# Windowed attention and two convolutions on one core: the maxima's transfer issued by ScalarE, and three engines' orders changed within a strip

## What is computed

```python
# first layer
x = layernorm2d(x0)                       # over the 96 channels of each pixel
q, k = conv1x1(x, qk_w)                   # 48 channels each
vs = conv1x1(x, vs_w)                     # 96 channels; v1 = first 48, v2 = last 48
local = depthwise_conv3x3(vs, depth_w)
q, k, v1 = roll(q, k, v1, by=-4 in both directions)
# windows of 8 x 8 pixels, 4 heads of 12 channels
y = softmax(q_window @ k_window.T * 12**-0.5) @ v_window
y = concat([roll_back(y), v2])
s = (y + local).mean(over the image)
ca = sigmoid(fu2 @ leaky_relu(fu1 @ s))
out0 = proj(y * ca + local * (1 - ca)) + x0
# second layer: pooled = out0.mean(); four taps per channel and image from pooled
out = depthwise_conv3x3(out0, taps(pooled), masked to the 4 taps above and left) + bias
```

## Time and profile before

| | before |
|---|---|
| runs | 1500.32 us median of 3 (1500.12 to 1502.79) |
| profiled execution | 1503.79 us, its span 1502.2 us |
| mean granted TensorE clock | 0.984 |
| PE / DVE / ACT / POOL busy, share of the span | 88% / 84% / 58% / 15% |
| DMA queue of SP | 202.60 MB, 53.9% of 16 engines' span |
| chain that ended last, largest parts | PE 36%, ACT 20%, DVE 16%, issue 13%, DMA 13% |

### The profile page before, as it was taken

How to read it: one execution, slowest core, us unless ns; L and a number is a source line. 1 busy time by engine, 2 the same in 40 slices (tenths; PEclk the granted TensorE clock), 3 DMA queues, 4 the chain that set the end, 5 groups by cost and what they waited for, 6 DMA issues and landing times.

```text
span 1502.2 us, 38208 instructions
## 1 busy us (share of the span) xinstructions
PE 1323.6 (88%) x12403; PEld 782.0 (52%) x12403; DVE 1263.8 (84%) x2222; ACT 875.8 (58%) x2279; POOL 230.8 (15%) x741
## 2 busy tenths in 40 slices
PE   5989898889899999989899999988989998888986
PEld 3666666555555555555555555555555555433332
DVE  3565656479999999999999999999989998999998
ACT  2566666666666666776566666765666666622221
POOL 2111111111122211221111211220112011000000
PEclk9999999999999999999999999999999999999999
DMA  2121212345665566645655566646655664678884
GB/s 62 51 82 55 81 55 81 99 98 148 167 148 144 138 152 165 156 114 154 166 147 139 138 159 156 156 114 159 155 125 141 161 155 112 164 181 195 211 199 126
DMA packets 81357, 203.07 MB, mean 135 GB/s; under 512 B 15248, under 2 KB 19112, under 8 KB 81320
## 3 DMA queue, kind: packets, MB, share of 16 engines
q1 hardware_dynamic: 81320, 202.60, 53.9%
HBM read 136.57 MB, written 64.91 MB: 134 GB/s over the span
## 4 chain that ended last, share of the span: by engine, by line
PE 36%; ACT 20%; DVE 16%; issue 13%; DMA 13%; ACTq 1%; DVEq 0%; SPq 0%; POOL 0%; POOLq 0%
DMA qd<-nmx 12%; PE banks_s L521 9%; ACT pt L811 5%; PE banks_t L529 5%; PE banks_t L483 5%; ACT km L767 4%; DVE mx L1009 4%; ACT ybuf L799 4%; PE banks_g L612 4%; PE banks_g L496 4%; DVE mixed L1181 3%; PE banks_g L614 3%; DVE oo L1192 3%; ACT vw L780 2%; DVE zs L1204 2%
## 5 line engine op out<-in xcount | busy, mean ns | idle before, releaser
L1181 DVE SCALAR_TENSOR_TENSOR mixed<-vin,c_pack,mixed 96x1024 f32<-96x1024 f32 x352 | 450.0, 1278 | 6.6
L1192 DVE SCALAR_TENSOR_TENSOR oo<-zs,l_w,oo 96x1024 f32<-96x1024 f32 x192 | 245.1, 1276 | 8.3 <-ACT oo L847 4.1
L811 ACT ACTIVATE pt<-banks_t 128x512 f32<-128x512 f32 x256 | 138.6, 593 | 129.0 <-PE banks_t L529 127.5
L1009 DVE TENSOR_REDUCE mx<-banks_s 128x8 f32<-128x512 f32 x260 | 167.6, 687 | 48.1 <-PE banks_s L521 47.3
L529 PE MATMUL banks_t<-qd,km 64*128 64x128 f32 x2048 | 152.8, 290 | 30.1 <-DMA qd<-nmx 30.0
L521 PE MATMUL banks_s<-km,qd 64*128 64x128 f32 x2080 | 152.9, 286 | 18.9 <-issue 15.2
L980 DVE BATCH_NORM_STATS2 bn<-banks_a 128x6 f32<-128x96 f32 x528 | 99.0, 249 | 80.5 <-PE banks_a L471 80.1
L521 PEld LDWEIGHTS banks_s<-km,qd 64*128 64x128 f32 x2080 | 129.7, 189 | 70.7 <-DVE mx L1009 40.4
L612 PE MATMUL banks_g<-vin,proj_t 128*96 128x512 f32 (+1 forms) x288 | 150.2, 622 | 11.4 <-DMA ycat<-y_img 5.7
L529 PEld LDWEIGHTS banks_t<-qd,km 64*128 64x128 f32 x2048 | 127.9, 192 | 49.9 <-issue 26.1
L434 POOL COPY vrow<-vw 96x16 f32<-96x16 f32 (+2 forms) x520 | 153.4, 349 | 0.0
(11 more groups left out here) (148 smaller groups left out, 1842.5 us busy)
## 6 DMA issues: line engine op xcount, KB each, us to landing
vin<-v_img SPq DMA_DIRECT2D x64, 495.0 KB, 5.9
v_img<-vrow SPq DMA_DIRECT2D x130, 198.0 KB, 2.8
xc<-in_x SPq DMA_DIRECT2D x134, 192.0 KB, 2.6
x<-in_x SPq DMA_DIRECT2D x64, 384.0 KB, 7.2
out<-oo SPq DMA_DIRECT2D x64, 384.0 KB, 3.0
y_img<-ybuf SPq DMA_DIRECT2D x128, 99.0 KB, 2.0
ycat<-v_img SPq DMA_DIRECT2D x64, 198.0 KB, 4.9
ycat<-y_img SPq DMA_DIRECT2D x64, 198.0 KB, 7.0
```

The lines of the kernel that those rows point to most:

```text
L811: fn(pt[:, 2 * r + n, :], banks_t[:, n, :], ACT.Exp).then_inc(pt_done, 1)
L1009: v.tensor_reduce(mx[:, n, :, 4 * r:4 * r + 4].rearrange("q h e -> q e h"), banks_s[:, n, :].rearrange("q (e h k) -> q e h k", h=2, k=K), ...
L1181: v.scalar_tensor_tensor(out=mb[:C, par, :, 0:W], in0=vin[:C, par, 1 + dh:1 + dh + WS, 1 + dw:1 + dw + W], scalar=depth_w[:, DVE_TAPS[m]:D ...
L1192: v.scalar_tensor_tensor(out=oo[:, par, :, :], in0=zs[:, at:at + WS, 1 + dw:1 + dw + W], scalar=l1_w[:, n:n + 1], in1=oo[:, par, :, :], op ...
```

## The change

In `strip`, the DMA of the maxima is issued by ScalarE right behind the instruction that writes them, and no more by SP behind the loads; `alone` keeps SP for it. On PE, x_transposed 1 moves up behind vs_of, project 0 goes ahead of scores 0, values 1 ahead of scores 1, and max_transposed behind project 1 (in a `gated` strip it stays ahead of it). On ACT, rsqrt goes ahead of keys. On DVE, statistics 1 and variance go ahead of mix 2, maxima 0 behind l1 (1), maxima 1 behind mix 5, and each `maxima` is one instruction over both banks; the counts on `mx_done` are halved.

```diff
@@ -343,7 +343,7 @@
 
-            def strip(h, k, attend=True, y=True, ahead=False, prev=False, older=False, gate=None):
+            def strip(h, k, attend=True, y=True, ahead=False, prev=False, older=False, gate=None, alone=False):
 
@@ -367,14 +367,14 @@
                     load_strip(t - LAG + 1, k, prev, gate)
-                if attend:
+                if attend and alone:
                     move_max(t + 1, 1 - k)
 
-            strip(0, 0, y=False)
-            strip(0, 1)
+            strip(0, 0, y=False, alone=True)
+            strip(0, 1, alone=True)
             with sp.Fori(1, NS // 2) as h:
-                strip(h, 0)
-                strip(h, 1)
+                strip(h, 0, alone=True)
+                strip(h, 1, alone=True)
             sp.wait_ge(rim_stored, 16 * 2 * B)
@@ -531,7 +531,7 @@
             def max_transposed(s):
-                pe.wait_ge(mx_done, 4 * (s + 1))
+                pe.wait_ge(mx_done, 2 * (s + 1))
                 nc.tensor.transpose(ps_mx, mx[:].rearrange("q t h p -> q (t h p)"), ident[:]).then_inc(mt_done, 1)
@@ -589,7 +589,7 @@
             scores(0, 0)
-            pe.wait_ge(mx_done, 2)
+            pe.wait_ge(mx_done, 1)
             scores(0, 1)
@@ -640,7 +640,7 @@
                 values(t, k, 0, not y)
-                pe.wait_ge(mx_done, 4 * (t + 1) + 2)
+                pe.wait_ge(mx_done, 2 * (t + 1) + 1)
                 scores(1 - k, 1)
@@ -659,6 +659,7 @@
                     vs_of(t + 1)
+                    x_transposed(t + 2, k, h + 1, 1)
                 elif prev:
@@ -672,35 +673,36 @@
                 if attend:
-                    x_transposed(t + 2, k, h + 1, 1)
                     keys_queries(t + 1)
...
                     pe.wait_ge(km_done, 2 * (t + 2))
-                    pe.wait_ge(qd_done, 2 * (t + 2))
-                    pe.wait_ge(nmx_done, t + 1)
                 if gated is not None:
                     pe.wait_ge(mid_act, gated + 1)
-                if attend:
-                    scores(1 - k, 0)
-                if gated is not None:
                     pe.wait_ge(proj_done, N_PROJ * (gated + 1) - 2)
...
                     project(u, um, par, 0, tail)
+                if attend:
+                    pe.wait_ge(qd_done, 2 * (t + 2))
+                    pe.wait_ge(nmx_done, t + 1)
+                    scores(1 - k, 0)
                 if gate is not None and not attend:
...
                 if attend:
-                    pe.wait_ge(mx_done, 4 * (t + 1) + 2)
+                    values(t, k, 1, not y)
+                    pe.wait_ge(mx_done, 2 * (t + 1) + 1)
                     scores(1 - k, 1)
-                    values(t, k, 1, not y)
                     pe.wait_ge(yq_done, FREE + 2 * t + 1)
-                    max_transposed(t + 1)
                 if gated is not None:
+                    if attend:
+                        max_transposed(t + 1)
                     one_column(gated, projT[:], st[:, 12:13], 3, C, 3)
...
                     project(u, um, par, 1, tail)
+                if attend and gated is None:
+                    max_transposed(t + 1)
                 if gate is not None and not attend:
@@ -800,10 +802,12 @@
 
-            def maxima_out(s):
+            def maxima_out(s, k):
                 act.wait_ge(mt_done, s + 1)
...
                 fn(nmx[:], ps_mx, ACT.Copy, scale=-1.0).then_inc(nmx_done, 1)
+                act.wait_ge(nmx_done, s + 1)
+                act.dma_start(qd[62:66, k, :, :, :].rearrange("j p w q -> j (p w q)"), nmx[:]).then_inc(mx_moved, 16)
 
@@ -916,8 +920,8 @@
                         sigmoid_exp(gated)
+                    rsqrt(t + 2)
                     keys(t + 1, 1 - k)
-                    rsqrt(t + 2)
                     queries(t + 1, 1 - k)
@@ -931,7 +935,7 @@
                 if attend:
-                    maxima_out(t + 1)
+                    maxima_out(t + 1, 1 - k)
                 if ahead:
@@ -1005,10 +1009,9 @@
                     dve.wait_ge(mt_done, s)
-                for n in range(2):
-                    v.tensor_reduce(mx[:, n, :, 4 * r:4 * r + 4].rearrange("q h e -> q e h"),
-                                    banks_s[:, n, :].rearrange("q (e h k) -> q e h k", h=2, k=K),
-                                    AX.X, ALU.max).then_inc(mx_done, 1)
+                v.tensor_reduce(mx[:, :, :, 4 * r:4 * r + 4].rearrange("q n h e -> q n e h"),
+                                banks_s[:, :, :].rearrange("q n (e h k) -> q n e h k", h=2, k=K),
+                                AX.X, ALU.max).then_inc(mx_done, 1)
 
@@ -1243,13 +1246,13 @@
                     mix(u, par, 1, tail)
+                if attend:
+                    statistics(t + 2, 1)
+                    variance(t + 2)
                 if gated is not None and attend:
...
                     mix(u, par, 2, tail)
-                if attend:
-                    statistics(t + 2, 1)
-                    variance(t + 2)
                 if gated is not None and attend:
@@ -1261,16 +1264,17 @@
                     normalise(t + 2, k, 1)
-                    maxima(t + 1, 0)
                 if gate is not None and not attend:
...
                 if attend:
-                    maxima(t + 1, 1)
+                    maxima(t + 1, 0)
                 if cur and not tail:
                     mix(u, par, 5, tail)
+                if attend:
+                    maxima(t + 1, 1)
                 if gate is not None and not attend:
```

## The result

The changed kernel takes **1555.43 us** (median of 4, 1547.86 to 1556.14) against 1500.32: ratio 1.035, 95% interval 1.032 to 1.039. It was forecast at 1472 us, in a range of 1456 to 1511. It lost 55 us, nearly twice the 28 that were forecast as a gain.

The account below looks back on a forecast made before the run. PE and DVE nearly full, the period closed by a loop through both and the maxima's DMA; 42 inner strips times (21.1 - 20.3) = 34, less 6, plus 1: 29 us, 1475, median 3.5 lower: 1472 us, range 1456 to 1511.

Parts of the forecast that it names:

- the loop from `finish` through l1 (1), maxima 0 and scores 1: PE and DVE, one inner strip: 14.25 us to scores 1 plus 5.68 to the next `finish`, 19.93, say 20.0.
- The new wait for maxima 0: PE ahead of scores 1: waits some 0.5 us because maxima 0 now comes behind l1 (1).
- the cover for ACT's issue: ACT ahead of exps 0: issuing the transfer takes 0.69 us there and is covered by 0.5 us.
- A merged maxima: DVE: one instruction takes between 1.19 and 1.28 us, a gain of 0 to 0.09 us each time.
- rival 1: At scores_transposed 0, the transfer takes the place of the waits removed: 1509 us, or 1547 at 4.62 us; chance 0.2.
- L: Time from issue to landing of the maxima's transfer on ScalarE: taken as 2.8 us, between 2.0 and 3.7.
- from above: Upper bound on L: the transfer still lands behind the loads, 21.1 us behind scores_transposed, so 3.7 us.
- The 0.47 us that PE waited: PE ahead of scores_transposed, before: its only wait for the 4.62 us DMA, since PE works meanwhile.
- Its queue was not late: SP's queue: SP loses one wait per strip by the change, and was not late before.
- y_out 0.25 us later: ACT: y_transposed goes half a microsecond later, y_out had 0.35 us to spare, so all behind it comes 0.25 later.
- 6 us forecast: Loss in the three gated strips, 2 us net for each.
- 2 was taken: Each gated strip: maxima 0 comes about 2.4 us later, taken as a net loss of 2 us.

Follow-up runs that it names:

- e3: Changed kernel with SP's load of x0 held until the transfer of the maxima has landed; 1463 us, ratio 0.974 to before.
- e8: e3 with the three gated strips in the old order of scores 0 and maxima 0; 1455 us, ratio 0.964 to before.
- e16: Changed kernel with gated strips in the old order and, except in those, the loads at the head of SP's strip; 1464 us, ratio 0.972 to before.
- e11: e8 with each maxima as the pair of instructions of before; 1459 us, ratio 0.969 to before.
- e15: Kernel before with the seven loads at the head of SP's strip, ahead of the store of y, except in gated strips; 1479 us, ratio 0.983.
- e13: Changed kernel with one unused matmul ahead of PE's wait for the transfer of the maxima; 1538 us, ratio 1.025 to before.
- e14: e13 with the three gated strips in the old order of scores 0 and maxima 0; 1528 us, ratio 1.017 to before.
- e10: Changed kernel with y_transposed ahead of x_transposed 1 again; 1534 us, ratio 1.016 to before.
- e2: Changed kernel with the issue of the maxima's transfer given back to SP behind the loads; 1573 us, ratio 1.047 to before.
- e1: Kernel before, all orders old, with only the issue of the maxima's transfer moved to ScalarE; 1501 us, ratio 1.000.

## Why the prediction was wrong

**What held.** The orders of PE and DVE. With the transfer fast, the loop from `finish` through l1 (1), maxima 0 and scores 1 gives 19.93 to 19.95 us (e3, e8, e16), where the working had 19.93, said 20.0. That isn't luck: its two terms, `finish` to scores 1 and scores 1 to the next `finish`, measure 14.14 and 5.80 us in e3, where it had 14.25 and 5.68. The new wait for maxima 0 is 0.64 us for 0.5, and the cover for ACT's issue came as written. A merged maxima takes 1.22 us as written; what it gains couldn't be told from nothing (e11). The decisive point of rival 1, L from 3.5 on, held too.

**What failed: the size of L.** The step was "I take 2.8, about the middle between 2.0 and 3.7: little of the loads is left by then". The chain's median is 3.92. By the prediction's own sum that alone makes a period of 21.4 us and a time of about 1519 (an estimate), so it explains 46 of the 83 us by which the forecast was off. No row stood behind a middle, and both rows from inner strips, 4.62 and 6.14, lay beyond it. The step "from above" did have the mechanism: landing behind the loads some 21.1 us behind scores_transposed. But it was taken as a bound on L, where it is a period: before, the strip was 20.9 to 21.4 us because that loop takes so long. The 0.47 us that PE waited were its sign. Nothing in the change shortens it: the engines' idle pieces that the reorder fills weren't on it. "Its queue was not late", said of SP, was the same mistake. e15 shows the other side, 1.7% faster with no order of PE, DVE or ACT changed.

**What lengthened it.** The prediction had y_out 0.25 us later and nothing for POOL. At full clock y_out's delay comes to 0.09 us at SP's loads of x, while SP's new waits for POOL's copies are 15.1 us in e13, 0.4 us a strip.

**What was missing: the clock.** The sum had no term for it. Later transfers made PE's waits longer, up to 3.4 us, and 102 us of the stage ran at half clock instead of 17. e13 puts it at 0.26 us an inner strip, some 10 us in all, and 14.5 more in the boundaries.

**The boundaries** were mis-sized: 6 us forecast, 26 measured. Of these, 14.5 went when the clock held (e13). The order of the gated strips gives 2.9 us each where the transfer is fast (e8) and 1.7 where it isn't (e14); 2 was taken. With the transfer fast and this order old, the boundaries stand at 180.4 us in e8, 3 above before; in e16 they stand at 190.1, because of the wait of 10.2 us at the first.

Against before, an inner strip lost 0.75 us: 0.26 for the clock by e13, and 0.49 that stay at full clock, of which the later issue of x0 (13.90 to 14.43 us) is the whole. Of that, 0.4 is SP's wait for POOL. What y_transposed's place does in e10 goes with these copies: it brings their end forward and the wait is gone. Rival 1 was the case that came, beyond its near end of 1509 and even beyond its 1547, and only 0.05 had been given to it beyond 1511.

## What to carry to other kernels

Ask of a wait how its time comes about, not how it can be overtaken: a DMA that takes 4.6 us where the same one takes 2.0 in a quiet stage stands behind something, and if that is issued at a fixed distance behind the instruction that waits, period and loop are the same length. Look in SP's queue for what each issue waits for, back to the engine that starts it, before any engine is reordered; here the place of the loads was worth 1.7% alone and made the new orders worth their 0.6 us a strip. Follow the engines that seem idle too: POOL was busy for 19% of the span and still held SP up. And move nothing late onto a transfer that PE already waits for: what such a wait can cost beyond itself is TensorE's clock.

## What the runs showed of the hardware

- The granted clock was halved behind waits of PE of 1.96 and of 1.53 us, and kept behind ones of 1.07, 1.54 and 2.22, all in the changed kernel. At the lower level sixteen matmuls took 2.00 us for 1.16 and the next four 2.73 for 1.96.
- A transfer of 16 KB from ScalarE's own queue landed 3.2 to 5.3 us after its issue behind 384 KB of SP's in the changed kernel, and within 2.13 without them in the strip of e3 shown. From SP's queue it took 0.3 us more there (e2); at the old place in the order the two queues made no difference (e1).
- POOL's copies of 96x256 took 0.42 to 0.45 us, and 1.43 to 1.51 beside a `scalar_tensor_tensor` of 96x1024 on DVE. Over the whole kernel the mean of a copy of v (L434) rose from 349 to 528 ns by the change.
